# Dense attention, layer 0: the value matmuls ahead of the next head's maxima within a half step

## The reference

```
norm = 1.0 / np.sqrt(KEY_DIM)
Q = jnp.einsum('bsd,hdk->hbsk', q, W_query)
K = jnp.einsum('bsd,hdk->hbsk', q, W_key)
V = jnp.einsum('bsd,hdv->hbsv', q, W_val)
scores = norm * jnp.einsum('hbqk,hbnk->hbqn', Q, K)
attn = jax.nn.softmax(scores, axis=-1)
heads = jnp.einsum('hbqn,hbnv->hbqv', attn, V)
out = jnp.einsum('hbqv,hve->bqe', heads, W_out)
```

## Time and profile before

| | us |
|---|---|
| median of 3 runs | 2007.82 |
| lowest, highest | 2007.16, 2022.02 |
| the profiled execution | 2016.01 |
| its span, first to last instruction | 2014.3 |
| TensorE busy, of the span | 1210.0 |
| VectorE busy | 1333.2 |
| ScalarE busy | 809.7 |
| GpSimd busy | 257.7 |

### The profile page before, as it was taken

How to read it: one execution, slowest core, us unless ns; L and a number is a source line. 1 busy time by engine, 2 the same in 40 slices (tenths; PEclk the granted TensorE clock), 3 DMA queues, 4 the chain that set the end, 5 groups by cost and what they waited for, 6 DMA issues and landing times. The chain is left out here.

```text
span 2014.3 us, 28534 instructions
## 1 busy us (share of the span) xinstructions
PE 1210.0 (60%) x10381; PEld 600.2 (30%) x10382; DVE 1333.2 (66%) x2983; ACT 809.7 (40%) x1520; POOL 257.7 (13%) x257
## 2 busy tenths in 40 slices
PE   6379999999999984659542530403027856621144
PEld 4112222222222232559431310201024535420033
DVE  3699999999999905454442258586755755577711
ACT  2139889889888983122100220300014223410021
POOL 2200000000000000133015330100123200000033
PEclk9569999999999996679955765756557968855567
DMA  1201111111111000000053310000035432110012
GB/s 61 37 11 18 24 28 18 20 28 22 18 26 26 2 2 13 17 1 1 1 159 98 85 26 0 0 0 0 0 84 127 50 66 34 38 52 1 0 47 58
DMA packets 52679, 65.43 MB, mean 32 GB/s; under 512 B 12296, under 2 KB 39948, under 8 KB 52269
## 3 DMA queue, kind: packets, MB, share of 16 engines
q1 hardware_dynamic: 47899, 56.31, 13.7%
q0 software_dynamic: 3840, 5.93, 1.2%
q10 hardware_dynamic: 800, 1.38, 0.3%
HBM read 36.76 MB, written 13.63 MB: 25 GB/s over the span
## 5 line engine op out<-in xcount | busy, mean ns | idle before, releaser
L598 ACT ACTIVATE l0att_probs<-l0att_ps_sv 128x512 f32<-128x512 f32 x1024 | 555.3, 594 | 115.3 <-PE l0att_ps_sv L578 106.2
L633 DVE TENSOR_REDUCE l0att_half_negmax<-l0att_ps_m 128x1 f32<-128x1024 f32 x480 | 548.4, 1213 | 9.2 <-PE l0att_ps_m L522 9.2
L547 PE MATMUL l0att_ps_sv<-l0att_probs,l_V_aug 128*32 128x256 f32 x4096 | 334.3, 393 | 0.0
L578 PE MATMUL l0att_ps_sv<-l_Q,l_K 51*128 51x512 bf16 x1024 | 201.2, 390 | 16.6 <-ACT l0att_probs L598 14.5
L522 PE MATMUL l0att_ps_m<-l_K,l_Q 48*128 48x512 bf16 x960 | 186.3, 386 | 19.8 <-DVE l0att_half_negmax L633 14.7
L547 PEld LDWEIGHTS l0att_ps_sv<-l0att_probs,l_V_aug 128*32 128x32 f32 x4096 | 89.3, 108 | 195.3 <-issue 108.8
L578 PEld LDWEIGHTS l0att_ps_sv<-l_Q,l_K 51*128 51x128 bf16 x1024 | 49.1, 93 | 232.7 <-ACT l0att_probs L598 220.8
L257 PE MATMUL ada_ps<-ident_sb,xn 128*128 128x128 f32 x128 | 34.5, 464 | 138.8 <-DVE xn L250 138.8
L2359 ACT ACTIVATE l3loc_probs<-l3loc_ps_s 128x320 f32<-128x320 f32 x128 | 49.0, 435 | 85.9 <-PE l3loc_ps_s L2340 85.4
L311 POOL CAST l0att_nm<-l0att_negmax 128x16 bf16<-128x16 f32 x16 | 3.2, 198 | 547.5 <-DVE l0att_negmax L610 547.5
L2536 PE MATMUL l3sel_ps_c<-l3sel_part,l3sel_ones 128*128 128x15 bf16 x56 | 10.9, 194 | 99.3 <-DVE l3sel_part L2561 99.3
(11 more groups left out here) (557 smaller groups left out, 2243.2 us busy)
## 6 DMA issues: line engine op xcount, KB each, us to landing
l_Q<-l_qp SPq DMA_DIRECT2D x184, 32.0 KB
l_K<-l_kp SPq DMA_DIRECT2D x184, 32.0 KB
l3f_mlp_l_w<-in_l_w_dram SPq DMA_DIRECT2D x2, 2048.0 KB
l_sorted_in<-l1ffn_zeros SPq DMA_DIRECT2D x1, 3072.0 KB
l1exp_rows<-l_sorted_in SPq DMA_DIRECT2D x4, 768.0 KB, 7.0
l_sorted_out<-l1exp_y SPq DMA_DIRECT2D x4, 768.0 KB, 5.6
l_Q<-in_local_mask_q_dram SPq DMA_DIRECT2D x2, 1170.0 KB
l_K<-in_local_mask_k_dram SPq DMA_DIRECT2D x2, 1170.0 KB
```

The costliest lines, as they stand in the source:

```text
L547: mm = pe.matmul(ps_v[32 * c:32 * c + 32, cols], V_aug[:, kt, h, :], probs[:, kt % 2, c, cols], start=(kt == 0 and part == 0), stop=(kt == ...
L578: pe.matmul(ps_s[:, (n + i) % 3, :], K[at, h % HEAD_BUFS, c1(kt)], Q[at, h % HEAD_BUFS, c4(2 * pair + i)], start=True, stop=True).then_inc ...
L598: act.activation(probs[:, kt % 2, c, :], ps_s[:, n % 3, :], ACT.Exp).then_inc(expd, 1)
L633: dve.tensor_reduce(half_negmax[:, h % 2, t, half:half + 1], src, AX_X, ALU.max, negate=True).then_inc(m_read, 1)
```

## The change

The three lines of the half step are put in another order: the values of the key tile before are issued directly behind the pair of scores, and the turns (maxima, and where they stand in the plan the transposes) behind the values. No instruction is added or removed, and no semaphore, buffer or wait changes; each wait is still in front of the instruction that had it.

```diff
@@ -578,10 +578,10 @@
                                 pe.matmul(ps_s[:, (n + i) % 3, :], K[at, h % HEAD_BUFS, c1(kt)],
                                           Q[at, h % HEAD_BUFS, c4(2 * pair + i)], start=True,
                                           stop=True).then_inc(scored[i], 1)
+                            if kt >= 1:
+                                values(h, kt - 1, pair)
                             while todo and (pair == 1 or len(todo) > len(plan[h, kt]) // 2):
                                 run(todo.pop(0))
-                            if kt >= 1:
-                                values(h, kt - 1, pair)
                     for part in range(2):
                         values(h, NT - 1, part)
                 run(("pv", L0_H - 1))
```

## The result

| | before | after |
|---|---|---|
| median of 10 runs, us | 2015.89 | 2024.12 |
| lowest to highest | 2005.86 to 2022.42 | 2015.58 to 2036.32 |
| the profiled execution | 2016.01 | 2031.63 |
| its span | 2014.3 | 2029.9 |

Ratio of times 1.0054, 95% interval 1.0028 to 1.0079: slower by half a per cent, inside the 1% that was called no change. The forecast was 2021 against the 2007.82 then known, a difference of 13.3 us and a ratio of 1.0066, within the interval. That 2021 is so near to 2024.12 is partly luck: over ten runs the kernel before has a median 8.1 us above the one over three from which the forecast counted. In the two profiled executions the spans differ by 15.6 us.

What follows compares the result with a forecast made beforehand. VectorE was taken to bound the kernel at 2.26 us per key tile, TensorE at 2.34 after the change. Head 38.73 + 0.59 + 0.52 = 39.84 against 38.99; +13.3 us in all on 2007.82 gives 2021, range 2005 to 2036.

Steps and rivals of the forecast that it cites:

- The wait that opens: Pair 0 of each key tile: values (V) wait for the fourth exponential; key tile 2.34 us on TensorE, not 2.22.
- V to M 0.57: TensorE, each half step: a maximum (M) starts 0.57 us after one part of the values (V); price unknown beforehand.
- M to S 0.23: TensorE, each half step: the next pair of scores (S) starts 0.23 us after a maximum (M); 0.23 to 0.31 possible.
- Rival A: Values to maxima: M's weights load while V streams, gap below 0.49 us, not slower, say 2001 us; chance 0.12.
- rival C: Pair 0 of each key tile: maximum to scores costs 0.31 us, 17 us more, 2039 us; chance 0.08.
- rival B: Key tile: exponentials run ahead, the fourth is no longer late, VectorE's 2.26 us rules, no effect, 2008 us; chance 0.10.
- Who is the bound: Key tile: VectorE at 2.26 us bounds the kernel before; TensorE, waiting for ScalarE, at 2.34 the changed one.
- Transposed maxima: Key tile 14: the maximum waits for a buffer VectorE still reads, 0.52 us more per head, bounds 0 and 1.05.
- Transposes of the output: Key tile 3: four transposes and what follows take 0.59 us per head, upper bound 0.67.
- The sum over heads: Heads 1 to 13 +11.1 us, head 0 +0.7, head 14 +1.3, head 15 at most 0.2; sum +13.3.
- rival D: TensorE's clock: falls to 1.2 GHz for one head because TensorE stands still a little, 28 us more, 2049 us; chance 0.03.

Runs made afterwards that it cites:

- e3: Changed kernel with every exponential over 256 of its 512 columns, both value parts reading those: head 38.23 us, key tile 2.22.
- e9: Changed kernel with a third buffer for the exponentials and each value part issued half a step later: heads 38.95, 40.5 or 42.0 us, ratio 1.0039 to the kernel before.
- e6: Changed kernel with VectorE reducing only 512 of each maximum's 1024 columns: head 39.32 us, key tile 2.33.
- e11: Kernel before with values ahead of maxima in pair 0 alone, VectorE reducing 512 of each maximum's 1024 columns: head 39.54 us, key tile 2.33.
- e5: Kernel before with VectorE reducing only 512 of each maximum's 1024 columns: head 37.82 us, key tile 2.22.
- e2: Kernel before with values ahead of the maxima in pair 1 alone: head 40.82 us, ratio 1.0122 to the kernel before.
- e1: Kernel before with values ahead of the maxima in pair 0 alone: head 39.98 us, ratio 1.0084 to the kernel before.
- e4: Kernel before with each head's first maximum issued at the end of the head before, VectorE's copy behind it: head 38.99 us, ratio 1.0007.
- e8: Kernel before with e4's early maximum and all turns up to the output's transposes moved half a step ahead: head 38.55 us, ratio 0.9936.
- e10: e9 with the turns spread as in e8: heads 39.27, 40.8 or 42.2 us, ratio 1.0022 to the kernel before.

## Why the prediction was right, step by step

- *The wait that opens.* Right in place and size: key tile 2.33 for the forecast 2.34, shown by e3 and e9 (take the exponential's lateness away, it goes; in e9 with everything computed) and by e6 and e11 (take VectorE away, it stays). That head 14 of the old trace held the new sequence is what made the size readable beforehand.
- *V to M 0.57, M to S 0.23.* Right, 405.14, 405.71 and 405.94 above. Rival A (the drain closes) and rival C (M to S 0.31) are thereby out, and rival B by the 0.75 of V. The rule of the Trainium skill (TensorE: Matmul & The Clock Gate, step 1 of what happens at a matmul) that weight loads are pulled ahead of running matmuls, weighed under A, did not close the gap between values and maxima: M's weights load at 405.71, with M. Between maxima and scores, equal shapes, the trace agrees with it: S's weights load at 405.89, while M runs and 0.05 ahead of S.
- *Who is the bound.* Right (e5, e6).
- *Transposed maxima.* 0.62 (444.38 - 443.76) for 0.52: the reading ahead of it started 0.57 behind its M, not the 0.46 of the row used, since VectorE was still reading the M before. Transposes of the output as forecast (0.59); head 39.78 for 39.84.
- *The sum over heads.* Heads 1 to 13: 13 x 0.79 = 10.3 (forecast 11.1). Head 0: the half clock lasted one half step longer (S at 137.85 is still followed 1.98 later by the next at 139.83; before, it was 1.34 there), so +1.35 for +0.7. Head 14 +1.15 for +1.3. Head 15 +0.9 for at most 0.2: its key tiles 1 and 2 ran partly at the lower clock, rival D for a few us, and all of the 0.9 is there:

```profile
728.00:732.00 4.00, 3.32 (x28) 0.94 (x30) 0.00 (x0) 3.71 (x8) 0.00 (x0) 0.81 0.01 2
732.00:736.00 4.00, 4.00 (x38) 1.18 (x34) 0.28 (x2) 3.01 (x6) 0.00 (x0) 0.76 0.02 4
```

Errors of both signs; 13.6 measured in the stage for 13.3 forecast is closer than its parts deserve. The 0.9 of head 15 is not shown to come from the change: key tiles 0 to 2 of head 15 have no turns, so the order of the matmuls there is the same before and after. Without it the stage would have lost 12.7. What no part of the forecast had is that the spacing of the maxima is itself a constraint (e2): the change as made keeps them nearly even (1.11 and 1.22), its halves do not.

What stays open: why the clock fell in head 15 of the changed kernel and of e6, and not in e1, e2 and e11, which have the same matmuls in the same order in these key tiles; and why in e9 it fell in six heads of 13 that all start alike.

## What to carry to other kernels

When two independent blocks of one in-order queue are swapped, ask which wait the first block was covering; here maxima that put V 0.54 instead of 0.31 behind S hid a fourth exponential, and the old trace had a place where the cover was already missing, which gave the price. Work that feeds another engine through two buffers wants even spacing: in this stage gaps of 0.45 and 1.77 us cost 0.11 us in a key tile and 1.8 us in a head, against gaps of 1.11 and 1.11, though the sum of work was the same. And an idle gap of the bounding engine is only won when the supply behind it is moved too (e4 against e8).

## What the runs showed of the hardware that was not expected

In e9, heads 1 to 13 start with three half steps without values (TensorE busy 1.89 of 3 us). In six of the 13 this was followed by the 1.2 GHz level, which cost 1.5 us in five of them and 3 in one; in e10, with the same start, in three of 13. The others kept the clock, and so did every head 1 to 13 of the kernels before and after, with two such half steps. It did follow two such half steps at the start of head 15, in the changed kernel and in e6. Moving values away from the head's start took 0.83 us off a head (38.95 for 39.78) and lost on average 0.8 to the clock (10.5 us in 13 heads).
